# A graph layer on one core: gathering batches ahead of the message products on TensorE, edge rows in four places, and a gather ring that shrinks in two steps

## What is computed

```python
def _mlp(h, W, b, gamma, beta):
    h = relu(h @ W + b)
    mu = mean(h, axis=0); var = mean(square(h - mu), axis=0)
    return gamma * (h - mu) * rsqrt(var + EPS) + beta
h = maximum(_layernorm(x), 0)
node_feat = _mlp(h, W_node, b_node, g_node, beta_node)
edge_feat = _mlp(edge_attr, W_edge, b_edge, g_edge, beta_edge)
message = _mlp(concatenate([h[src], h[dst], edge_feat], axis=1), W_msg, b_msg, g_msg, beta_msg)
out = x + segment_sum(message, dst, num_segments=N) + node_feat
```

## Time and profile before

| | |
|---|---|
| median of 3 runs | 996.21 us (996.05 to 1000.87) |
| the profiled execution | 996.7 us, of it 994.9 us span |
| PE busy | 774.8 us, 78% of the span |
| GpSimd busy | 716.9 us, 72% |
| VectorE busy | 662.0 us, 67% |
| ScalarE busy | 381.6 us, 38% |
| mean granted TensorE clock | 0.911 of full speed |

### The profile page before, as it was taken

How to read it: one execution, slowest core, us unless ns; L and a number is a source line. 1 busy time by engine, 2 the same in 40 slices (tenths; PEclk the granted TensorE clock), 3 DMA queues, 4 the chain that set the end, 5 groups by cost and what they waited for, 6 DMA issues and landing times.

```text
span 994.9 us, 21739 instructions
## 1 busy us (share of the span) xinstructions
PE 774.8 (78%) x4750; PEld 624.3 (63%) x4822; DVE 662.0 (67%) x1590; ACT 381.6 (38%) x648; POOL 716.9 (72%) x762
## 2 busy tenths in 40 slices
PE   1734687567258898888788789899989999987898
PEld 1604562222148787787777778777777777776684
DVE  8577878778735555555577756767766766665555
ACT  2843696667323333333444433222222222222230
POOL 6777777777777777774777777777777777777750
PEclk9957795766569999999999999999999999999999
DMA  9575533333633333333444333232323233222223
GB/s 296 132 283 156 127 73 80 77 74 80 166 68 74 73 72 76 74 74 67 92 101 102 80 85 70 63 76 64 66 65 76 64 67 76 65 63 64 57 56 98
DMA packets 102661, 91.30 MB, mean 92 GB/s; under 512 B 73638, under 2 KB 78390, under 8 KB 102409
## 3 DMA queue, kind: packets, MB, share of 16 engines
q1 hardware_dynamic: 76144, 51.04, 19.2%
q0 software_dynamic: 24256, 37.31, 17.4%
q10 hardware_dynamic: 2136, 1.62, 0.6%
HBM read 72.00 MB, written 14.54 MB: 87 GB/s over the span
## 4 chain that ended last, share of the span: by engine, by line
SPq 29%; PE 20%; issue 16%; POOL 11%; DMA 9%; DVE 8%; ACT 4%; ACTq 3%; DVEq 0%; POOLq 0%
SPq L581 14%; POOL ring L625 11%; PE pd L972 6%; SPq L529 4%; DMA xs<-x_stack 4%; PE pc L961 4%; PE pb L984 3%; DMA ring<-p_table,src_idx 3%; SPq L574 3%; PE pc L859 3%; SPq L515 2%; DVE ring L1313 2%; ACTq L806 2%; DMA big_a<-zeros 2%; SPq L404 2%
## 5 line engine op out<-in xcount | busy, mean ns | idle before, releaser
L625 POOL DMA_INDIRECT ring<-p_table,src_idx x710 | 670.9, 945 | 226.7 <-issue 196.4
L972 PE MATMUL pd<-hm 128*97 128x193 f32 x1564 | 295.2, 331 | 0.9 <-ACT hm L792 0.9
L972 PEld LDWEIGHTS pd<-hm 128*97 128x97 f32 x1564 | 247.9, 167 | 5.1 <-ACT hm L792 1.2
L961 PE MATMUL pc<-w3q,r_sb 128*128 128x96 f32 x1564 | 208.3, 277 | 46.3 <-DMA xs<-x_stack 16.4
L961 PEld LDWEIGHTS pc<-w3q,r_sb 128*128 128x128 f32 x1564 | 204.0, 194 | 52.2 <-ACT r_sb L782 26.1
L782 ACT ACTIVATE r_sb<-pa 128x512 f32<-128x512 f32 x196 | 116.7, 596 | 305.6 <-issue 163.8
L1268 DVE TENSOR_TENSOR gram<-gram,pd 97x97 f32<-97x97 f32 x196 | 50.2, 256 | 163.7 <-PE pd L972 149.8
L792 ACT ACTIVATE hm<-pc 128x384 f32<-128x384 f32 x196 | 96.2, 491 | 156.9 <-DVE pc L1262 149.3
L1262 DVE TENSOR_TENSOR pc<-pc,ring 128x384 f32<-128x384 f32 x194 | 108.6, 560 | 61.2 <-PE pc L961 32.0
L1165 DVE BATCH_NORM_STATS2 edge_st<-r_sb 96x512 f32 (+1 forms) x196 | 121.3, 675 | 36.1 <-ACT r_sb L744 34.7
L984 PE MATMUL pb<-ring 128*128 128x288 bf16 x784 | 114.2, 290 | 24.5 <-DVE ring L1313 24.4
(11 more groups left out here) (125 smaller groups left out, 494.7 us busy)
## 6 DMA issues: line engine op xcount, KB each, us to landing
w3q<-q_table SPq DMA_DIRECT2D x782, 11.2 KB
ring<-p_table,src_idx POOLq DMA_INDIRECT x710
ln_buf<-p_table ACTq DMA_DIRECT2D x704, 0.4 KB
xs<-x_stack SPq DMA_DIRECT2D x98, 72.0 KB
x_stack<-ring SPq DMA_DIRECT2D x6, 980.0 KB, 5.6
xs<-x_stack SPq DMA_DIRECT2D x98, 60.0 KB
ln_buf<-p_table SPq DMA_DIRECT2D x320, 0.4 KB
ring<-in_x_nodes SPq DMA_DIRECT2D x5, 480.0 KB, 9.1
```

The costliest lines, as they stand in the source:

```text
L625: nc.gpsimd.indirect_dma_start(out=ring[:, tile * C:(tile + 1) * C], out_offset=None, in_=table, in_offset=bass.IndirectOffsetOnAxis(ap=id ...
L961: last = nc.tensor.matmul(pc[:, j % 2, t * C:(t + 1) * C], r_sb[:, j % 2, t * TILE:(t + 1) * TILE], w3q[:, j, t, :], start=True, stop=True)
L972: last = nc.tensor.matmul(pd[0:M1, j % 2, 0:HW], hm[:, j, t, WIN:HW], hm[:, j, t, :], start=(t == 0), stop=(t == n - 1))
```

## The change

Four things are changed.

1. **TensorE's order.** In a body the gathering batches stand ahead of `products(g + 1)`, no longer behind it.
2. **Edge rows.** `xs` had four places for pairs of groups, of which the main stage used two. Now it uses all four, and SyncE issues the load of a pair four groups earlier; two more pairs are loaded before the first Q window.
3. **The ring.** It shrinks from 60 to `MID` = 37 and then to `LATE` = 29 places. Groups 60 to 96 use places 0 to 36 and wait for the group 60 before them, groups 97 to 125 wait for the group 37 before them, and groups from 126 on for the group 29 before them.
4. **The room of the near groups.** What lay in places 29 to 59 is laid out anew, `stage` shrinks from ten chunks to `STAGES` = 3, its load is issued one body later and waits until chunk c - 3 is finished (`low_made`), and the masks wait until group 96 has been added.

```diff
-LATE = 29
+MID, LATE = 37, 29
+STAGES = 3
...
         def slot(g):
 
-            return g if g < RING else (g - RING) % LATE
+            return g if g < RING else g - RING if g < RING + MID else (g - RING - MID) % LATE
+
+        def slot_freed(g):
+
+            return g + 1 - (RING if g < RING + MID else MID if g < RING + MID + LATE else LATE)
...
+        def stage(c):
+
+            return stages[:, c % STAGES, 0:min(PART_B, NN - c * PART_B), :]
...
+                def load_edges(pair):
+
+                    if pair < NG // 2:
+                        wait(sp, edge_lin, 2 * pair - 6)
+                        sp.dma_start(xs[0:KX, pair % 4, :], x_stack[:, bass.ts(pair, 2 * GROUP)]).then_inc(
+                            x_main[pair % 4], 16)
+
+                load_edges(0)
+                load_edges(1)
                 for g in range(NG):
                     i, j = at(0, g)
                     if g % 2 == 0:
-
-                        wait(sp, edge_lin, g - 2)
-                        sp.dma_start(xs[0:KX, j // 2, :], x_stack[:, g * GROUP:(g + 2) * GROUP]).then_inc(
-                            x_main[j // 2], 16)
+                        load_edges(g // 2 + 2)
...
-                    for c in part_step(g, -3):
+                    for c in part_step(g, -2):
                         sp.wait_ge(pre_added, RING)
+                        wait(sp, low_made, c + 1 - STAGES)
...
-                        wait(pool, pre_added, g + 1 - (RING if g < RING + LATE else LATE))
+                        wait(pool, pre_added, slot_freed(g))
...
                     for j in range(BODY):
                         edges(i, j + 2)
+                        for n in near_turns(num(i, j)):
+                            gather_near(n)
                         products(i, j + 1)
                         if isinstance(i, int) and num(i, j) >= NG - 2:
 
                             keep_clock(W_GATHER[num(i, j) - (NG - 2)])
-                        for n in near_turns(num(i, j)):
-                            gather_near(n)
                         window_sum(i, j)
...
                         dve.wait_ge(near_placed, tile // TPG + 1)
+                        dve.wait_ge(low_made, PARTS)
+                        dve.wait_ge(pre_added, RING + MID)
```

More of the change, by code:

```diff
@@ L122, in graph_layer @@
         late = ring[:, LATE * TPG * C:RING * TPG * C]
[L123 to L128, removed]
+        parts_at, stage_at = late.shape[1] - NN * 3 * C // 2, (MID - LATE) * TPG * C
+        parts = late[:, parts_at:].bitcast(bf16).rearrange("p (b s c) -> p b s c", s=3, c=C)
+        stages = late[:, stage_at:stage_at + STAGES * PART_B * C].rearrange("p (k b c) -> p k b c", k=STAGES, c=C)
+        near_at = HOT_BUFS * HOT_B * P // 2
+        hots = late[:, 0:near_at].bitcast(bf16).rearrange("p (k b e) -> p k b e", k=HOT_BUFS, b=HOT_B)
+        near_f = late[:, near_at:near_at + 2 * GROUP].rearrange("p (k e) -> p k e", k=2)
         near_src = late[:, near_at:near_at + 2 * GROUP].bitcast(i32).rearrange("p (k e) -> p k e", k=2)
-        near_f = late[:, near_at:near_at + 2 * GROUP].rearrange("p (k e) -> p k e", k=2)
         near_at += 2 * GROUP
         near = late[:, near_at:near_at + NEAR_T * C]
+        assert near_at + NEAR_T * C <= parts_at and stage_at + STAGES * PART_B * C <= parts_at
         big_a = sb("big_a", [P, NP])
@@ L267, in graph_layer @@
         near_made = sem("near_made")
-        x_main = [sem(f"x_main{k}") for k in range(2)]
+        x_main = [sem(f"x_main{k}") for k in range(4)]
         q_in = [sem(f"q_in{k}") for k in range(4)]
@@ L584, in _ @@
                         load_far(n)
-                    for c in part_step(g, -3):
+                    for c in part_step(g, -2):
                         sp.wait_ge(pre_added, RING)
+                        wait(sp, low_made, c + 1 - STAGES)
                         rows = p_table[c * PART_B * P:min((c + 1) * PART_B, NN) * P, :]
-                        sp.dma_start(stage[:, part_blocks(c), :], rows.rearrange("(b p) c -> p b c", p=P)).then_inc(
+                        sp.dma_start(stage(c), rows.rearrange("(b p) c -> p b c", p=P)).then_inc(
                             stage_in[c], 16)
@@ L817, in _ @@
                         act.wait_ge(stage_in[c], 16)
-                        nc.scalar.copy(parts[:, part_blocks(c), 0, :], stage[:, part_blocks(c), :]).then_inc(high_made, 1)
+                        nc.scalar.copy(parts[:, part_blocks(c), 0, :], stage(c)).then_inc(high_made, 1)
                     for c in part_step(g, 2):
                         act.wait_ge(high_off, c + 1)
-                        nc.scalar.copy(parts[:, part_blocks(c), 1, :], stage[:, part_blocks(c), :]).then_inc(mid_made, 1)
+                        nc.scalar.copy(parts[:, part_blocks(c), 1, :], stage(c)).then_inc(mid_made, 1)
                     for tile in near_tile(g + 2, 0):
@@ L1289, in near_parts @@
                         dve.wait_ge(part_copied, 2 * c + 1)
-                        V.tensor_tensor(stage[:, part_blocks(c), :], stage[:, part_blocks(c), :], part_scratch(c),
+                        V.tensor_tensor(stage(c), stage(c), part_scratch(c),
                                         ALU.subtract).then_inc(high_off, 1)
@@ L1295, in near_parts @@
                         dve.wait_ge(part_copied, 2 * c + 2)
-                        V.tensor_tensor(parts[:, part_blocks(c), 2, :], stage[:, part_blocks(c), :], part_scratch(c),
+                        V.tensor_tensor(parts[:, part_blocks(c), 2, :], stage(c), part_scratch(c),
                                         ALU.subtract).then_inc(low_made, 1)
```

5 lines of the change are left out of this document (3 added, 2 removed).

## The result

The changed kernel takes 1047.74 us (median of 4 runs), the kernel before 997.49 us (median of 4): a ratio of 1.0497, 95% interval 1.0467 to 1.0527. The profiled execution took 1047.9 us, its span is 1046.1 us. The forecast was 1040 us with a range of 1029 to 1051.

A forecast was written before the change was run, and what follows sets the result against it. SyncE's queue was taken to set the pace before the near stage, then TensorE and VectorE, GpSimd's gathers at its end. Group 185's sum 43.7 us later gave 996.7 + 43.7 = 1040.4, forecast 1040 us, range 1029 to 1051.

The forecast's parts named there:

- The ring: GpSimd's gathers: the stop near 450 us goes, no new one comes, every gather from group 89 on comes 10.1 us earlier.
- The order on TensorE: Near-stage bodies: batches still wait for masks, products stand in the open; one batch 4.73 us, two 5.72, a tile 24.29.
- the term of 55.7 us: Near stage on TensorE: 3.48 us more in each of sixteen tiles, 55.7 us more in all.
- Edge rows: SyncE's queue before the near stage: earlier loads make nothing faster, two extra loads cost little; taken as 0.
- one of the signs to look for: Start of the near stage in the changed profile: the sum of group 105 within 2 us of 604 us.
- SyncE's wait on `low_made`: SyncE's queue, chunk 3: met with about 3 us to spare, costs nothing; 17 us in all if the spare time were gone.
- What follows group 185: After the near stage: the time from group 185's sum to the end stays 46.0 us.
- The sum: Whole kernel: group 185 summed at 992.6 us instead of 948.94, 43.7 us later; span 1038.6 us.
- seven falls of the clock: TensorE's near stage: room in the range up to 1051 us for falls to half pace, each about 1.5 us.
- the faster one: Rival, near stage: products not behind the batch's wait, or masks there when the body opens; tile 20.9 us, 986 us, chance 0.06.
- The one on edge rows: Rival, stage before the near stage: earlier edge rows free up to 35.6 us of waits; 1005 to 1028 us, chance 0.08.
- The one on the clock: Rival, near stage: TensorE's 1.46 us idle in each of 64 bodies lowers its clock; above 1051 us, chance 0.08.

The follow-up runs named there:

- the kernel in which the conversions don't interfere: The changed kernel with ScalarE's conversion of the near groups' source numbers, and SyncE's load for it, one body earlier: 1041.81 us, ratio 1.0442 to the kernel before.
- early masks: The changed kernel with the masks of body g + 1 built at the head of VectorE's body g: 987.38 us, ratio 0.9875 to the kernel before.

## Why the prediction was right, and where its sizes were off

**The ring.** Right. The stop near 450 us went, no other came, and the last gathers are issued 10.4 us earlier. Alone it is worth 12.5 parts in a thousand (985.79 us). I had called 10.1 us the most that it can give; that was the stop in one profile, and where the old ring stands in other kernels the same stop was 13.05 us (the order alone) and 13.2 us (edge rows alone).

**The order on TensorE.** Right in mechanism and size. I had worked out 4.73 and 5.72 us for bodies with one and two batches and 2.40 for those without; the profile has 4.72, 5.72 and 2.40. Sixteen tiles of 24.29 us are 388.6 us; the kernel in which the conversions don't interfere took 388.7. The old order behind the same ring took 334.7, so the term of 55.7 us measures 54.0 without the conversions and 58.0 with them. The order alone gave the whole loss, and early masks took it away with the order in place.

**Left out: the tile starts.** The changed kernel needed 4.1 us more than that in the near stage (392.7 us). I had counted 0.1 us a tile. VectorE waited 2.1 us in all for conversions, 0.2 before; each such delay shows in full in its body, and once a fall of the clock stands behind it, which made that body 1.5 us longer still. I take it that the products, standing in front of the batches, would have covered most of a delay of 0.6 us; no kernel with the old order and the masks in their old place has a conversion that late (0.2 us at most), so this is argued and not shown.

**Edge rows.** Right that they win nothing while SyncE's queue sets the pace: alone the near stage began at 605.8 us, 1.9 later than before. I took the start of the near stage as unchanged, and had named a start within 2 us of 604 us as one of the signs to look for; it came at 609.5, the largest miss of the sum. Over all kernels with node rows on SyncE it lay between 603.9 and 611.1 us: 603.9, 604.3 and 607.5 with the old loads of edge rows, 604.2 to 611.1 in seven kernels with the early ones. Two loads more at the start (about 1 us) belong to the change. Whether the rest does, or is the scatter of a queue that issues without pause, these single profiles don't tell apart.

**SyncE's wait on `low_made`.** Right: nothing to be seen in the kernel with the ring and the layout alone.

**What follows group 185.** I kept 46.0 us; it took 43.9. The difference lies in body 186, which took 6.48 us before and 3.87 after. In the kernel before, its products waited 2.17 us for ScalarE's edge relu, and the window sum behind them ran at the lower level of the clock (timeline of TensorE):

```profile
951.28 1.66 PE L961 MATMUL pc<-w3q,r_sb 128*128 128x96 f32 x8 [2.17 <-ACT r_sb L782]
952.73 2.66 PE L972 MATMUL pd<-hm 128*97 128x193 f32 x8
```

In the changed kernel the same wait was 1.21 us, and the window sum took 1.48 us.

**The sum.** 5.6 + 47.7 - 2.1 = 51.2 us of span, where I had 43.7. The mechanism carried the forecast, but that 1047.74 us still lies inside 1029 to 1051 is partly luck: I had left the upper end for seven falls of the clock, one came, and what filled it was the late start, whose cause I can't name in full, and the conversions. The rivals: the faster one needed the masks to be there at the head of a body, and with the masks so placed the chip gave just its time, 986 us and a little more; TensorE kept its order in front of a waiting batch, and the weight loads of the products stayed behind it too (in body 146 no weight load starts between 804.03 and 806.54 us, and those of the products follow at 809.32). The one on edge rows fell with its kernel. The one on the clock did not hold, since the granted clock of the near stage was 1.00 with 1.3 us of idle time or more in each of 64 bodies. By the Trainium skill ("TensorE: Matmul & The Clock Gate", section "A second HAM failure mode: psum-queue depth-cycling") frequent short idle times can make the clock swing; here the trace doesn't agree: one fall of the clock in the near stage, behind one idle time of 1.98 us.

## What to carry to other kernels

Before an instruction is moved ahead on an in-order engine, ask what it waits for and whether that comes any earlier: if not, what it passes loses its cover, and its full duration is added in every turn. The order made no difference that could be measured once the producer on the other engine stood early enough, so the place of the producer is the one to move, with an eye on what that producer then waits for itself. A wait named after a load may belong to the queue that issues it; loading earlier in the same queue only renames the wait.

## What the runs showed of the hardware

Short idle times that repeat did not lower the clock: about 1.3 us of idle time in a body of 4.72 or 5.72 us, in nearly all of 64 bodies, at a granted clock of 1.00. Single longer ones sometimes did. Idle times of 1.98 us (body 146), 2.17 us (body 186 before) and 2.41 us were followed by work at the lower level, but 1.96 us (body 126) and 2.34 us (body 166) in the near stage of the changed kernel were not. No run here shows what decides between them.

Taking about 0.4 us of issue out of every second pair of groups in SyncE's queue brought group 105 forward by 12 us on average (three kernels at 592.2 to 597.2 us, ten at 603.9 to 611.1), and those issue times come to about 11. Kernels with the same loads in SyncE's queue differ by up to 7 us among themselves at this point, so a single pair of profiles, such as the one that gives 18.9 us, is not enough to size such a gain.
